# Edge counts of a graph layer with two one-hot buffers and one pair of edge rows per loop turn

## The reference, cut to what matters

```python
# src, dst: 21,250 edges (20,000 random ones and 1,250 loops), sorted by dst
e = leaky_relu(s_src[src] + s_dst[dst], 0.2)
alpha = softmax of e over the edges with the same dst
out = segment_sum(alpha[:, :, None] * h[src], dst)
# as the kernel has it: count[d, s] = number of edges from s to d,
# and log(count) is added to the dense scores before the softmax
```

## Time and profile before

| what | value |
|---|---|
| median of three runs | 2224.91 us |
| the profiled execution's own time | 2222.94 us |
| its span | 2221.2 us |
| mean granted TensorE clock | 0.938 |
| PE / DVE / ACT / POOL busy, share of the span | 89% / 52% / 27% / 26% |

### The profile page before, as it was taken

One profiled execution on the slowest core, in us unless ns is written; L12 is line 12 of the kernel. 1 busy time (PEld: TensorE's weight loads), 2 busy tenths in 40 slices (PEclk: granted clock), 3 DMA queues, 4 the chain that ended last, 5 costly groups with the idle time before them and its releaser, 6 DMA issues.

```text
span 2221.2 us, 28335 instructions
## 1 busy us (share of the span) xinstructions
PE 1969.1 (89%) x10975; PEld 1857.1 (84%) x10975; DVE 1154.6 (52%) x2051; ACT 595.4 (27%) x1176; POOL 576.4 (26%) x409
## 2 busy tenths in 40 slices
PE   4567888789997749999999999999997999999995
PEld 3344588689987749997889999999996999999995
DVE  5666513488867623337775334334355544374357
ACT  2332201278867513212242001001033010010012
POOL 1423252102100005322134214214204142142135
PEclk8688899889998869999999999999998999999997
DMA  3210132011101223100231111101013110120012
GB/s 124 90 60 33 41 109 68 23 39 49 56 24 67 101 91 113 50 1 22 76 113 57 29 29 58 30 28 58 15 50 97 31 57 30 36 72 29 29 43 111
DMA packets 74476, 124.32 MB, mean 56 GB/s; under 512 B 3297, under 2 KB 45065, under 8 KB 74348
## 3 DMA queue, kind: packets, MB, share of 16 engines
q1 hardware_dynamic: 74348, 122.59, 17.2%
HBM read 97.12 MB, written 25.45 MB: 55 GB/s over the span
## 4 chain that ended last, share of the span: by engine, by line
PE 66%; DMA 7%; DVE 6%; ACT 4%; issue 3%; POOL 1%; SPq 0%; DVEq 0%; ACTq 0%; POOLq 0%
PE pb L905 22%; PE pa L571 21%; PE pb L571 9%; PE pb L702 3%; DMA wt_d<-xu 3%; PE pb L813 2%; PE pa L689 2%; PE pa L702 2%; DMA md<-md_d 1%; DMA xg_d<-xw 1%; PE pb L720 1%; ACT sm L1260 1%; DVE st L1786 1%; ACT o1h L1285 1%; PE pa L782 1%
## 5 line engine op out<-in xcount | busy, mean ns | idle before, releaser
L905 PE MATMUL pb<-X_hi,uw_hi 128*128 128x416 f32 (+1 forms) x864 | 306.2, 354 | 6.0 <-issue 6.0
L905 PE MATMUL pb<-X_hi,uw_lo 128*128 128x416 f32 (+1 forms) x864 | 305.6, 354 | 0.0
L905 PE MATMUL pb<-X_lo,uw_hi 128*128 128x416 f32 (+1 forms) x864 | 305.5, 354 | 0.0
L1450 ACT ACTIVATE tr<-pb,V 128x418 f32<-128x418 f32 (+1 forms) x144 | 87.9, 610 | 769.5 <-PE pb L905 769.5
L571 PE MATMUL pa<-dw_hi,hh 128*125 128x384 f32 x960 | 246.4, 338 | 0.7 <-ACT tr L1450 0.7
L571 PE MATMUL pa<-dw_hi,hl 128*125 128x384 f32 x960 | 245.9, 337 | 0.0
L571 PE MATMUL pa<-dw_lo,hh 128*125 128x384 f32 x960 | 245.9, 337 | 0.0
L1840 DVE CAST hh<-tr 128x418 fp32r<-128x418 f32 (+1 forms) x144 | 115.3, 800 | 222.6 <-ACT tr L1450 222.6
L1023 POOL CAST uw_hi<-raw 128x768 fp32r<-128x768 f32 x48 | 42.9, 893 | 701.9 <-PE pb L905 612.0
L571 PEld LDWEIGHTS pa<-dw_hi,hh 128*125 128x125 f32 x960 | 172.4, 185 | 1.1 <-ACT tr L1450 1.1
L571 PEld LDWEIGHTS pa<-dw_lo,hh 128*125 128x125 f32 x960 | 172.9, 185 | 0.0
(11 more groups left out here) (344 smaller groups left out, 3759.3 us busy)
## 6 DMA issues: line engine op xcount, KB each, us to landing
raw<-in_L_mix_fc_w SPq DMA_DIRECT2D x48, 384.0 KB, 3.3
raw<-in_L_ffn_w SPq DMA_DIRECT2D x48, 384.0 KB, 3.3
md<-md_d SPq DMA_DIRECT2D x20, 610.4 KB
md_d<-mds SPq DMA_DIRECT2D x10, 610.4 KB
raw<-in_L_mix_qkv_w SPq DMA_DIRECT2D x24, 192.0 KB, 4.9
TOK<-in_x SPq DMA_DIRECT2D x10, 375.0 KB
xn_d<-TOK SPq DMA_DIRECT2D x10, 375.0 KB
xu<-in_x SPq DMA_DIRECT2D x10, 375.0 KB
```

The costliest lines, as they stand in the source:

```text
L905: last = nc.tensor.matmul(pb[:, j % 4, 0:n], w_[:, kk, :], x_[:, kk, o:o + n], start=(kk == 0 and q == 0), stop=(kk == KT - 1 and q == 2))
L1450: last = A_(RE[f"tr{j % 3}"][:, 0:w], pb[:, j % 4, 0:w], ACT.Identity if func == "mish" else func, bias=bias(b))
```

## The change

The ring has two buffers in place of four. A turn of the loop is one pair of edge rows, so two slots, on both engines. The number of turns of a tile is the number of its pairs, not half of it rounded up; two of the three column instructions that rounded go away.

```diff
-RING = 4
+RING = 2
@@ edge_counts (PE)
-                loops = pe.value_load(bnd[0:1, NT + t:NT + t + 1], min_val=1, max_val=EW // 2)
-                before = pe.value_load(bnd[0:1, 2 * NT + t:2 * NT + t + 1], min_val=0, max_val=NT * EW // 2)
+                loops = pe.value_load(bnd[0:1, NT + t:NT + t + 1], min_val=1, max_val=EW)
+                before = pe.value_load(bnd[0:1, 2 * NT + t:2 * NT + t + 1], min_val=0, max_val=NT * EW)
@@ bounds (DVE)
-            ch.link(v.tensor_scalar(bc[:, 4:5], bc[:, 3:4], 0.5, 0.25, ALU.mult, ALU.add))
-            ch.link(v.tensor_scalar(bc[:, 5:6], bc[:, 4:5], 8388608.0, None, ALU.add))
-            v.tensor_scalar(bc[:, 2:3], bc[:, 5:6], -8388608.0, None, ALU.add).then_inc(sem("e_bc"), 1)
+            v.tensor_scalar(bc[:, 2:3], bc[:, 3:4], 1.0, None, ALU.mult).then_inc(sem("e_bc"), 1)
@@ one_hots (DVE)
-                loops = dve.value_load(bnd[0:1, NT + t:NT + t + 1], min_val=1, max_val=EW // 2)
-                before = dve.value_load(bnd[0:1, 2 * NT + t:2 * NT + t + 1], min_val=0, max_val=NT * EW // 2)
+                loops = dve.value_load(bnd[0:1, NT + t:NT + t + 1], min_val=1, max_val=EW)
+                before = dve.value_load(bnd[0:1, 2 * NT + t:2 * NT + t + 1], min_val=0, max_val=NT * EW)
                 with dve.Fori(0, loops) as p:
                     for q in range(RING):
-                        first = 2 * p + p0 + q // 2
+                        first = p + p0
                         dve.wait_ge(*at(f"oh_used{q}", p + before + 1))
                         v.tensor_scalar(RM[f"D1h{q}"][:], RM["iota"][:, columns(t)],
-                                        ec[:, ds(first + (2 + q % 2) * EW, 1)], None, ALU.is_equal)
-                        v.tensor_scalar(RM[f"S1h{q}"][:], RM["iota"][:], ec[:, ds(first + (q % 2) * EW, 1)], None, ALU.is_equal
+                                        ec[:, ds(first + (2 + q) * EW, 1)], None, ALU.is_equal)
+                        v.tensor_scalar(RM[f"S1h{q}"][:], RM["iota"][:], ec[:, ds(first + q * EW, 1)], None, ALU.is_equal
                                         ).then_inc(sem(f"oh{q}"), 1)
```

## The result

| | before | after |
|---|---|---|
| median | 2225.10 us (4 runs) | 2258.18 us (4 runs, 2257.27 to 2260.05) |
| ratio | | 1.0144, 95% interval 1.0123 to 1.0166 |
| span of the profiled execution | 2221.2 us | 2257.4 us |
| the ten edge loops, first matmul to D1z | 154.4 us | 191.2 us |

The changed kernel is slower by 33.1 us in the median; 2256 was forecast, in 2241 to 2274.

What follows compares the result with a forecast made beforehand. DVE was taken to bound the edge loops at 0.62 us a slot, PE close behind. Two-buffer turns of 1.77 us, less slots saved, added 33.3 us over tiles 1 to 9 to 2222.94: 2256 us, range 2241 to 2274.

Steps and rivals of the forecast that it cites:

- Where it acts: Edge loops, 154.4 of 2221.2 us: tiles in series to the end, except tile 0, where up to some 6 us is hidden.
- The slot count: Edge loops: 188 slots in place of 200; ten of the twelve saved are on the path, worth 6.2 us at most.
- The ring: Two buffers between DVE and PE: a two-slot turn takes one buffer round, 1.77 us, or 0.88 a slot against 0.62.
- the head of a turn: Term of the buffer round: from PE's end of a slot to DVE's next D1h at a turn's start, 0.26 us.
- the lower bound, 1.66: Turn time in us if the simpler address makes the head of a turn as short as its inside.
- Turns and the loop's end (D): 94 turns for 50: loop-end work, 0.38 us on DVE, hidden. Rival: exposed, 2.15 us a turn, 2283 us, chance 0.05.
- POOL: While POOL splits pages it holds DVE's one-hots, so two buffers cost nothing more; spares about seven slots of tile 1.
- The sum: Growth of the loops of tiles 1 to 9, added tile by tile: 33.3 us, giving 2256 us.
- the forecast's own range: About 2256 us: shorter head of a turn -7, clock and POOL stretches +-5, given as 2244 to 2268.
- The clock (C): Rival, PE in the edge loops: clock stays low, slots cost 1.16 us, +35 us more, 2291 us; chance 0.06.
- A: Rival, edge loops: the buffer's return is hidden and only the slot count matters, 6.2 us faster, 2217 us; chance 0.05.
- B: Rival: the edge stage's length is hidden elsewhere, no change, 2223 us; chance 0.04.

Runs made afterwards that it cites:

- e6: e2 with the loop counts of the next tile read early as in e5 (four buffers, 188 slots); 2220.40 us, ratio 0.9980.
- e5: Kernel before, with the next tile's loop counts read into registers right behind the current tile's loop on both engines; 2216.54 us, ratio 0.9964.
- e2: Kernel before with four buffers, but both engines branch around a turn's second pair where a tile has no more (188 slots); 2233.95 us, ratio 1.0030.
- e1: Kernel before (50 turns of four slots, 200 slots) with only the depth cut, two buffers in place of four; 2271.59 us, ratio 1.0199.
- e3: Changed kernel with one matmul in place of three per slot, leaving out the counts of two thirds of the sources; 2239.64 us, ratio 1.0054.
- e7: Changed kernel with S1h computed for 418 of 1254 columns, PE's work as before, counts wrong; 2239.26 us, ratio 1.0068.
- e4: Changed kernel with one more wait, so POOL starts tile 0's subtraction only when PE has closed tile 1; 2259.12 us, ratio 1.0138.
- e8: Kernel before with one matmul in place of three per slot, the control for e3; 2215.44 us, ratio 0.9955.

## Why the prediction was right, point by point

**Where it acts.** Right: tile 0's growth stayed in the slack of the token DMA, and all other tiles are in series. The end of the stage moved by 32.8 us, the growth of these loops less 1.0 us.

**The slot count.** 188 slots, right. At four buffers the slots saved took 5.8 us off the loops where POOL's pattern is the same on both sides (e6 against e5), close to the 6.2 forecast as "at most"; in e2 it was 3.3, with tile 1 in POOL's other pattern.

**The ring.** Right as a mechanism. e1 has the loss without the turns, and e3 and e7 show both parts of the round. The size was 5% off: 1.69 us against 1.77. The term that was mis-sized is the head of a turn, 0.26 us, of which some 0.1 was register work for an address that the change makes simpler; the lower bound, 1.66, was the better value. It took 0.8 to 1.1 us off each of tiles 2 to 4.

**Turns and the loop's end (D).** Hidden, as forecast: the turn is at the sum of the round's parts, with nothing left for 0.38 us.

**POOL.** This step failed: seven slots of tile 1 under POOL as before, with "two buffers cost nothing more". Four were made there (D1h at 54.78, 55.66, 58.43 and 61.20), because a slot cost 2.77 us and not 1.71: before, two DVE instructions passed for each of POOL's; after, one did. POOL got through its pages sooner (bu ended at 64.7 us, before at 66.5), but five slots were left behind them and not two, and the last ran into the subtraction, which e4 prices at 2.2 us. Tile 1 grew by 5.5 us and not 2. As e2 falls into the same pattern with four buffers, part of this need not come from the ring; whether the change brought it on or only the moment at which POOL began is not shown. Tiles 6 and 7 also grew by 0.7 and 0.4 us more than forecast. In tile 6 POOL held the same D1h and S1h for the same time before and after (1.79 and 1.14 us), so that is another cause, and it is open.

**The sum.** That it came out at 33.3 for 33.7 is in part luck: tiles 1, 6 and 7 were forecast 4.5 us too low together, the other six 4.1 us too high. Two small slips of the working did no harm. Before, thirteen slots and not fourteen had begun in tile 1 by 54.5 us. And the forecast's own range, -7 and +-5 about 2256, ends at 2261 and not at 2268.

**The clock (C).** It read 1.00 in the full stretch above, so C was wrong for this change. e3, where PE has one matmul a slot, had it at 0.50 through the loop of tile 4. The Trainium skill, "TensorE: Matmul & The Clock Gate", section What's actually happening, says that the clock follows recent activity; e3 agrees with it by that 0.50; the changed kernel's loops did not come to that.

**A and B.** A fell with the round at 1.69 and B with the shift of 33 us.

**Behind the stage.** The profiled spans differ by 36.2 us, the medians by 33.1. POOL's xu is 33.3 us late; the other 2.9 us arise behind it in the one pair of profiled executions. Their cause was not looked for: it is inside the spread of the runs of the kernel before (2223 to 2232).

## What to carry to other kernels

What these runs show of a ring between two engines: four buffers hid the round of one buffer (writer's work, hand-over, reader's work, hand-over back), as four slots of 0.62 are 2.48 us and the round is 1.7; two did not, as two slots are 1.24. Add that round up from a lone slot in the trace before a buffer is taken away. By this sum three buffers (1.86 us) would still have done at the full clock; that is an estimate, and no run tries it. And look at the issue time at the head of a loop: reading its bounds one tile early was worth more here (8.4 us) than the slots saved (5.8 us of loops, lost again elsewhere).

## What the runs showed of the hardware that was not expected

- How DVE and POOL take turns has two patterns. One page on POOL, cast and subtraction, took 3.42 us with two slots between in the kernel before, e5, e6 and e8, and 2.77 us with one in the changed kernel, e1, e3, e4 and e2. DVE was busy for 7.30 of 7.30 us (57.40 to 64.70) in both the kernel before and the changed one, so idle time within the stretch is not it. In the runs with 3.42, POOL's first cast began beside an S1h that a D1h followed at once; in the others DVE had come to a D1h or a wait. What decides is not shown.
- The clock column can mislead at the start of a trace. In e8 it reads 1.00 in the loops of tiles 2 and 3 and 0.50 in that of tile 4, but a matmul takes 0.61 us in all of them. In tile 0 of e3 it reads 1.00 at 0.61 us as well. There the durations tell the level, and mean granted clocks (0.911 in e3, 0.936 in e8) do not compare.
- Reading a number into a register takes 0.30 us in the median on DVE, but up to 1.85 us in e2 and 1.78 in e5. Why a few of them are so long was not looked for.
- A branch and one more register read per tile cost more than the slots they saved: 5.8 us in the gaps between loops in e2, and some 4 us behind the stage (7.6 us between the medians less 3.9 in the stage).
